# The first norm of a small attention one unit earlier, and 12 instead of 9 low halves of the probabilities on GpSimd, in a Flamingo block

## What is computed

```python
def _L0_xattn_ref(x, context, w_q, w_k, w_v, w_o, b_o):      # 16 heads of 64
    q, k, v = x @ w_q, context @ w_k, context @ w_v           # by heads
    attn = softmax(einsum('bhid,bhjd->bhij', q, k) * SCALE)
    return einsum('bhij,bhjd->bhid', attn, v) @ w_o + b_o

def _L0_ffn_ref(X, norm1_w, norm2_w, wq, wk, wv, wo, ...):    # 16 heads of 8
    h = rmsnorm(X, norm1_w)
    attn = softmax(einsum('bshd,bthd->bhst', h @ wq, h @ wk) * scale)
    X = X + einsum('bhst,bthd->bshd', attn, h @ wv) @ wo
    h2 = rmsnorm(X, norm2_w)
    ...                                                       # router, top 2 of 8, experts, shared
    return X + moe_out

x = x + tanh(g_xattn) * _L0_xattn_ref(_layernorm(x), ctx, ...)
x = x + tanh(g_ffn) * _L0_ffn_ref(_layernorm(x), ...)
```

## The kernel before

| unit | 7 | 8 | 9 | 10 | 11 | 12 | 13 | 19 | 20 |
|---|---|---|---|---|---|---|---|---|---|
| steps | y1 p10 p11 | ln p12-14 | xf f0 p15 p16 | f1 p17 | f2 p18 | f3 p19 p20 | f4 f6 p21 | f14 p33-36 | y0 f15 p37 p38 |
| low half by | GpSimd | VectorE | GpSimd | VectorE | GpSimd | VectorE | GpSimd | VectorE | GpSimd |

## Time and profile before

### The profile page before, as it was taken

How to read it: one execution, slowest core, us unless ns; L and a number is a source line. 1 busy time by engine, 2 the same in 40 slices (tenths; PEclk the granted TensorE clock), 3 DMA queues, 4 the chain that set the end, 5 groups by cost and what they waited for, 6 DMA issues and landing times.

```text
span 1452.5 us, 34137 instructions
## 1 busy us (share of the span) xinstructions
PE 1291.5 (89%) x14216; PEld 927.8 (64%) x14216; DVE 997.7 (69%) x1825; ACT 803.3 (55%) x1220; POOL 667.2 (46%) x591
## 2 busy tenths in 40 slices
PE   4759999999999899999898989898999998868898
PEld 4146766676767676767576756666666666646676
DVE  2678676767676767686767676776767676846765
ACT  1034656565656565656565655556565656535644
POOL 3024444555554445454544544545453545443454
PEclk9579999999999999999999999999999999989999
DMA  7120302030302020212112020313030200000000
GB/s 220 34 59 13 73 12 74 12 73 13 73 13 68 14 66 17 60 22 45 37 28 58 13 73 12 73 13 73 13 73 12 58 12 14 13 14 1 8 7 11
DMA packets 122271, 57.19 MB, mean 39 GB/s; under 512 B 108262, under 2 KB 117706, under 8 KB 122122
## 3 DMA queue, kind: packets, MB, share of 16 engines
q1 hardware_dynamic: 122122, 55.07, 16.6%
HBM read 15.38 MB, written 0.82 MB: 11 GB/s over the span
## 4 chain that ended last, share of the span: by engine, by line
PE 57%; DVE 24%; ACT 7%; issue 5%; DMA 4%; POOL 2%; SPq 0%; DVEq 0%; ACTq 0%; POOLq 0%
PE psum L765 10%; DVE mx L1264 8%; PE psum L827 7%; PE psum L744 7%; PE psum L746 7%; PE psum L748 7%; DVE p_lo L435 6%; PE psum L780 4%; PE psum L856 3%; PE psum L869 3%; DMA cT_both<-c_new 3%; PE psum L819 3%; PE psum L793 3%; ACT p L966 3%; DVE kbd L1284 2%
## 5 line engine op out<-in xcount | busy, mean ns | idle before, releaser
L966 ACT ACTIVATE p<-psum 128x768 f32<-128x768 f32 (+1 forms) x384 | 321.3, 837 | 479.8 <-PE psum L748 479.6
L435 POOL TENSOR_TENSOR p_lo<-p,p_hi 128x768 f16<-128x768 f32 (+1 forms) x144 | 297.1, 2063 | 492.4 <-ACT p_hi L967 444.3
L1264 DVE TENSOR_REDUCE mx<-psum 128x1 f32<-128x512 f32 (+1 forms) x624 | 387.0, 654 | 83.8 <-PE psum L827 78.0
L765 PEld LDWEIGHTS psum<-c_both,p_hi 128*128 128x128 f16 x4992 | 286.2, 99 | 86.9 <-issue 34.7
L765 PE MATMUL psum<-c_both,p_hi 128*128 128x97 f16 (+1 forms) x4992 | 327.9, 207 | 6.9 <-ACT acc_sb L976 6.9
L967 ACT ACTIVATE p_hi<-psum 128x768 f16<-128x768 f32 (+1 forms) x384 | 319.4, 832 | 0.0
L827 PE MATMUL psum<-cT_both,qk_hi 96*128 96x512 f16 (+1 forms) x624 | 234.5, 387 | 66.1 <-DVE mx L1264 20.4
L435 DVE TENSOR_TENSOR p_lo<-p,p_hi 128x768 f16<-128x768 f32 (+1 forms) x240 | 260.8, 1087 | 25.5 <-ACT p_hi L967 24.8
L744 PE MATMUL psum<-qk_hi,cT_both 97*128 97x384 f16 (+1 forms) x768 | 195.2, 335 | 4.8 <-DMA qk_hi<-mrow 4.8
L746 PE MATMUL psum<-qk_lo,cT_both 96*128 96x384 f16 (+1 forms) x768 | 194.7, 334 | 0.0
L748 PE MATMUL psum<-qk_hi,cT_both 96*128 96x384 f16 (+1 forms) x768 | 193.5, 333 | 0.0
(11 more groups left out here) (188 smaller groups left out, 1848.3 us busy)
## 6 DMA issues: line engine op xcount, KB each, us to landing
c_both<-c_new SPq DMA_DIRECT2D x16, 768.0 KB, 4.8
ctx_nat<-in_ctx_dram SPq DMA_DIRECT2D x16, 528.0 KB
wg<-in_L_ffn_e_gate_dram SPq DMA_DIRECT2D x1, 1024.0 KB, 5.5
wu<-in_L_ffn_e_up_dram SPq DMA_DIRECT2D x1, 1024.0 KB, 7.8
wd<-in_L_ffn_e_down_dram SPq DMA_DIRECT2D x8, 128.0 KB, 5.4
aT<-a_new SPq DMA_TRANSPOSE x64, 2.9
out_dram<-x SPq DMA_DIRECT2D x4, 200.0 KB
x<-in_x_dram SPq DMA_DIRECT2D x1, 600.0 KB
```

The source lines that it names most:

```text
L435: engine.tensor_tensor(p_lo[0:m, i % 3, 0:w], p32[0:m, i % 3, 0:w], p_hi[0:m, i % 3, 0:w], ALU.subtract).then_inc(lo_made(b, i)[0], 1)
L765: t = mm(psum[:, ACCB + bank, k * (C + 1):k * (C + 1) + wide], p[0:m, i % 3, n * P:(n + 1) * P], c[parity][0:m, j, 0:wide], start=(j == 0 ...
L966: a(to32, src, ACT.Exp, scale=DH ** -0.5)
L1264: v.tensor_reduce(mx[:, rt, part:part + 1], bank[:, 0:w], AX.X, ALU.max)\
```

## The change

`ln` moves from unit 8 to 7, `xf` from unit 9 to 8, GpSimd's `norm_1` ahead of its low half of unit 7 instead of behind it, and the low halves of units 8, 10 and 12 go from VectorE to GpSimd.

```diff
-    plan[8].append(("ln", 0))
-    plan[9].append(("xf", 0))
+    plan[7].append(("ln", 0))
+    plan[8].append(("xf", 0))
...
-    CTX_AT, NORM1_AT, ACC0_AT, NORM2_AT = 0, 8, 14, 22
-    LO_POOL = (5, 7, 9, 11, 13, 16, 18, 20, 22)
+    CTX_AT, NORM1_AT, ACC0_AT, NORM2_AT = 0, 7, 14, 22
+    LO_POOL = (5, 7, 8, 9, 10, 11, 12, 13, 16, 18, 20, 22)
```

## The result

The changed kernel takes 1570.56 us, the median of 4 runs (1568.70 to 1574.32), beside 1459.00 us for the kernel before in the same runs: a ratio of 1.0757, 95% interval 1.0709 to 1.0805. It is slower; forecast were 1559 us, and slower with 0.92. The profiled execution is 1572.25 us with a span of 1570.5 us, 118.0 more than before.

A forecast was written before the change was run, and what follows sets the result against it. TensorE's queue was taken to set the time. 7.6 us in each of 14 middle batches (+106), first batch -2.5 and last -4 gave +100: 1554 us for the profiled execution, 1559 for the median, range 1505 to 1600.

The forecast's parts named there:

- L860's wait gone, a wait of about 5.4 us of L827 for `mx`.: In each middle batch the transposition stops waiting for `hn`, and p13's matmul waits about 5.4 us for p11's maximum.
- the walk: One middle batch followed in time from unit 7 at 624.16; without port cost, unit 10 starts 1.7 us later.
- The port, +2.7: Middle batches, behind the norm: GpSimd's halves of units 7 and 8 hold up `xf` and `hn`, +2.7 us a batch.
- Rival 2: First come, first served at the port: `xf` takes 0.35, the port costs 1.4 instead of 2.7; 1541 us, chance 0.13.
- The clock, +2.4: Middle batches: TensorE's stand of 5.4 us lowers the granted clock to half for 4.5 to 7 us, +2.4 us.
- rival 1: All as in the main case, but the clock stays up: +66, 1525 us, chance 0.12.
- Queue and placement, +2.5: Middle batches: `xf` and `hn` ahead of maxima, and p's moved between units, cost together +2.5 us a batch.
- The sum of a middle batch, +7.6: Queue and placement 2.5, port 2.7 and clock 2.4 make 7.6 us in each of 14 middle batches.
- The first batch, -2.5: First batch: no norm, three halves of 0.95 us off a nearly full VectorE, -2.5 us (0 to -3).
- The last batch, -4: Last batch: the statistics leave the place behind a weight split, `hn` ends near 1232.6 instead of 1236.4, -4 us.
- Rival 3: No port cost, and a stand of 2.7 us that seldom lowers the clock: 1487 to 1509 us, chance 0.10.
- rivals 4 and 5: Norm early enough, 1423 to 1440 us, chance 0.05; TensorE finds other work, nothing seen, 1445 to 1474 us, chance 0.03.

The follow-up runs named there:

- e3: The changed kernel, with GpSimd waiting for `hn` before it makes unit 7's half, so it is idle while VectorE scales: 1512.28 us, ratio 1.0336.
- e7: The changed kernel with GpSimd waiting for `hn` before unit 7's half and the p's in their units of before: 1482.49 us, ratio 1.0178.
- e10: e7 with 14 more matmuls of 384 columns ahead of p14 in the middle batches: 1465.45 us, ratio 0.9980.
- e4: The changed kernel with 30 more matmuls of 384 columns, no part of the computation, ahead of p13 in middle batches: 1536.91 us, ratio 1.0508.
- e8: The kernel before, with GpSimd waiting for `hn` ahead of the experts' inputs in the last batch: 1457.54 us, ratio 1.0000.
- e5: The changed kernel with the p's in the units in which they stood before: 1538.63 us, ratio 1.0550.

## Why the prediction was right, point by point

- **"L860's wait gone, a wait of about 5.4 us of L827 for `mx`."** Right: 5.3 us, with the walk's cause, p11's maximum behind `xf` and `hn`.
- **The port, +2.7.** Right: 2.75 by e3. The pairs of the last batch held for all the others. Rival 2 falls for this place: `xf` was started 0.04 us ahead of the half and lost in 14 of 14. First come, first served as such does not fall with it: with a lead of 0.10 us VectorE won in the last batches of e3, e7 and e10. The Trainium skill ("SBUF — State Buffer", Who interferes with whom) says that whichever issues first gets the shared pair of ports for the whole instruction. These runs agree with it at the 0.10 us lead; at 0.04 us the starts in the profile do not tell who came first, so the prediction read more out of the earlier trace rows than they hold, and had the outcome right. e3 shows that GpSimd's work beside the scalings is what makes them slow; that this is a matter of a port, no run here shows by itself.
- **The clock, +2.4.** Right: about 2.3 by e4. With this rival 1 falls, in which the clock stays up. But the 1.59 us of the first batch, on which the step leaned, was no firm sign: e8 has the same first batch and the same wait, and there the clock stayed up. TensorE and the clock in e8:

```profile
137.33 0.35 PE L827 MATMUL psum<-cT_both,qk_hi 96*128 96x420 f16 x1 [1.59 <-DVE mx L1264]
```

```profile
137.00:145.00 8.00, 7.22 (x80) 4.78 (x81) 7.17 (x12) 3.23 (x4) 1.76 (x1) 1.00 0.00 0
```
- **Queue and placement, +2.5.** About right in sum: of the 7.34 us of units 7 to 22, 2.75 are the port's and 2.1 the clock's (60.41 against 58.29 in e4), which leaves 2.5. Less so in its parts. Unit 11 is +1.63 (1.5), unit 13 +0.92 (0.9), unit 10 0.0 (-0.2), units 19 and 20 together -1.26 (-1.4). Units 7 to 9, where the walk had 1.7, are +2.45 with the port's cost taken out (e3), but that still holds a low clock in 11 of 14 batches; with the p's in their old units as well it is +1.67 (e7), and with the clock kept up +0.53 (e10). So the queue itself costs little, and 1.7 a batch, from e7 to e3, belongs to where the p's went. The prediction had 1.1 for the queue and 1.4 for the places (0.6 in unit 9, 0.8 in units 10 to 20).
- **The sum of a middle batch, +7.6.** Units 7 to 22 give +7.34 and the whole batch +7.95, 111.3 us in 14. The other 0.6 us lies in units 23 to 6, which no step of the sum has; they took 21.63 us before and 21.96 in e8, whose middle batches are the same, so half of it is within what executions differ by. The steps above lead from 53.07 over 53.58 (queue), 55.07 (its clock), 56.77 (places) to 60.41 (port and its clock). These steps were taken in one order; the clock's share is in two of them and its size depends on what else stands.
- **The first batch, -2.5.** Wrong: +0.9 from its first scores on (108.3 against 107.35 us). The step counted the halves that leave VectorE and not the p's that are placed anew: with the p's in their old units it is 104.9 (e5) to 105.3 us (e10), so that their new places put 3.4 on it. Nor do the halves show the gain that was forecast: 107.35 holds a stretch of 6.8 us at the low clock, and e8, with the same first batch and no such stretch, took 103.56 us, less than e5 and e10.
- **The last batch, -4.** Wrong: +4.2. The norm did come earlier (L860 11.34 us behind unit 7's start instead of 14.31, 3.0 instead of 4), but the inputs' subtraction now lay on L1114, and the clock was low for 34 us from there on, before 24. The gain did not reach the end: L882 comes 1.4 us later than before (49.4 against 48.0 us behind unit 7). The +4.2 itself is no firm number: e4 has the last batch of the changed kernel and took 230.4 us for it instead of 234.4, and e8 took 3.8 us more than before although a stand was shortened. A gain of 4 us is seen in neither; how much of the 8 us is the clock's was not separated.
- **The total.** 118 against 100 between the profiled executions: 5 from the middle batches, 5 from the first, 8 from the last. The median came out only 11.6 us above the forecast, because the profiled execution lay 1.7 us above this kernel's median, where the one before lay 4.9 below its own. Those 6.6 us are luck.
- **The other rivals.** Rival 3 (no port cost, the clock seldom down) falls by `xf` and `hn` at 1.76 and 1.67 us, rivals 4 and 5 (faster, nothing seen) by the stand of 5.3 us and the time.

## What to carry to other kernels

When a step is moved earlier, look at what its reader now stands in front of: here two scalings that waited for another engine were put ahead of maxima whose banks TensorE needed, and a wait of 1.1 us became one of 5.3. Give an idle engine more work only after asking what that work will lie beside: a GpSimd instruction behind the one that releases VectorE can cost VectorE its whole length, and one wait on a semaphore takes that away. Price a stand of TensorE with the clock behind it. And before a few us in one stretch are explained, look at the same stretch in a kernel that is alike there: here such pairs differed by 4 us.

## What the runs showed of the hardware

- A VectorE scaling and a GpSimd subtraction kept each other waiting. GpSimd won where VectorE was started 0.04 us ahead of it, and with two halves back to back it won again, so that two instructions of 0.35 us lasted until 3.23 us of GpSimd's work were done. VectorE won where it was started 0.10 us ahead, and the two halves took 3.63 instead of 3.24 us.
- Matmuls whose result nobody reads made the kernel faster: in the middle batches by 2.28 us each in e4, and by 1.49 us in units 7 to 22 in e10.
- The same wait did not always lower the clock: of the waits of about 2.2 us in e7 (one of each middle batch) nine were followed by a low clock and five were not, 1.60 us at L878 was followed by a low clock in e8 and not before, 1.59 us in the first batch before and not in e8. What decides this stayed open.
